# A decoder layer in float32: the first attention's work per tile re-ordered over two tiles, its layer norm moved to ScalarE

## The chip, the cores and the metric

The kernel is one program on one core of a Trainium2 chip. The metric is the device time of an execution in microseconds (us), from launch to end; the profiler takes one execution apart into the instructions of each engine. The engines are TensorE (PE, its weight loads PEld), VectorE (DVE), ScalarE (ACT), GpSimd (POOL) and SyncE (SP, which issues most DMAs). They run side by side and wait for each other on semaphores; each runs its own instructions in the order in which they are written.

## The reference, cut to what matters

The layer works on x of 16 x 64 tokens by 512. It is an attention with 32 heads of 16 and a layer norm, a cross-attention with 32 heads of 128 and a layer norm, and a gated dense layer with a layer norm. Only the first attention is touched by the change:

```python
xq = rotary((x @ Wq).reshape(b, s, 32, 16))
xk = rotary((x @ Wk).reshape(b, s, 8, 16));  xv = (x @ Wv).reshape(b, s, 8, 16)
xk, xv = repeat(xk, 4, axis=2), repeat(xv, 4, axis=2)
scores = einsum('bqhd,bkhd->bhqk', xq, xk) / sqrt(16)
probs = softmax(where(causal, scores, -inf), axis=-1)
x = layernorm(x + einsum('bhqk,bkhd->bqhd', probs, xv).reshape(b, s, 512) @ Wo)
```

Every product is computed to near float32 by splitting each operand into a rounded high part and the low rest and adding three products (high x high, high x low, low x high).

## The kernel before

**Tiles and steps.** The first attention runs over eight tiles of 128 tokens (two sequences of 64). Tile i's scores fall in four units of 512 columns (u = 0 to 3); two PSUM banks hold them, so units 0 and 1 are computed together, and then 2 and 3. The steps of one tile, with the names of the code:

- PE: `a_stage` turns the input tile over (four 128x128 transposes), `b_stage` multiplies by Wq (12 matmuls of 512 columns), `kv_stage` by Wk and Wv (12 of 256). `qk_stage` turns the rotated queries and keys over, six groups of four transposes (q, q, k, q, q, k) in three banks by turns. `s_stage` makes the scores of two units. `pt_stage` turns the probabilities of one unit over, `pv_stage` makes one half of the products with the values (24 matmuls of 256 for both halves), `wo_stage` multiplies by Wo (12 of 512), `x1_stage` turns the normed result over for the second attention.
- DVE: `rope_q` and `rope_k` (three instructions each) do the rotary products out of PSUM; `masked_max` is a COPY_PREDICATED that takes the masked scores out of PSUM and a TENSOR_REDUCE for the maxima; `total` is the sum of the exponentials and a RECIPROCAL; `add1` adds the residual from the bank of `wo_stage`; `stats1`, `moments1` and `norm1` are the layer norm; every `..._low` subtracts a high part from its source (L1379): `x_low`, `q_low` (1024 columns), `p_low` of one unit, `at_low` of the value products, `x1_low`.
- ACT: the high parts (all L885): `x_high`, the six copies of `qk_stage`'s banks, `p_high`, `at_high`, the 1024-column copy of the queries that feeds `q_low`, `x1_high`; and the exponentials (L923).
- POOL: `sub` (score minus maximum), `norm` (times the reciprocal), the two sums that end the rotary step (`t1q + t2q`, L1234, and the same for k), the low part of the keys (L1241) and of the values (L1252), and the inverse root of the norm (`root1`).
- SP: loads and the shuffling of the values.

**What sets the order.** No planner: each engine has a function `tile_steps(i)` written out by hand, with semaphore waits in front of each step. Work of three tiles stands in it: i (named `i`), v = i - 1 and w = i - 2. Tiles 0, 1 and 7 are unrolled and tiles 2 to 6 are a hardware loop. In PE's `tile_steps(i)` the steps stand as b(i), pt(v,0), pt(v,1), kv(i), pt(v,2), pt(v,3), a(i+1), qk(i), scores(i; 0,1), pv(v) in full, x1(w), scores(i; 2,3), wo(v). Behind tile 7 comes a hand-written passage into the second attention: pt(7,0), pt(7,1), four query products of the second attention (48 matmuls of 256 columns), pt(7,2), pt(7,3), pv(7), wo(7) and so on; the second attention's 32 units and the dense layer follow.

## Time and profile before

| | us |
|---|---|
| median of 3 runs (lowest to highest) | 824.31 (824.14 to 825.51) |
| the profiled execution, its own time | 824.27 |
| its span, first to last instruction | 822.5 |
| mean granted TensorE clock, share of full speed | 0.988 |
| busy over the span: PE / PEld | 765.3 (93%) / 691.1 (84%) |
| busy: DVE / POOL / ACT | 623.6 (76%) / 391.8 (48%) / 319.4 (39%) |

The busy shares are averages over stages that differ. The first attention takes the stretch from about 20 to 186 us; the rest belongs to the loads ahead of it and the two later stages. PE's busy time is modelled from pipelined matmuls, so a stretch can read as busy while its matmuls start later than they could; the start times of steps tell more than the busy column.

### The profile page before, as it was taken

To read this page: it belongs to the slowest core of one execution; us is meant where nothing else is said; L and a number is where in the kernel's file an instruction comes from. 1 tells how busy PE (TensorE), PEld (TensorE's weight loads), DVE (VectorE), ACT (ScalarE), POOL (GpSimd) and SP (SyncE) were. 2 spreads that over 40 slices of the span, in tenths; PEclk is the share of its full clock that TensorE was granted. 3 is DMA by queue.
4 is the path that set the end of the run, shared out by engine and by line. 5 is a ranking of instruction groups with operands and counts; after the bars stand their busy time and mean duration, and the time that the engine had idled before them with its cause. 6 is when DMAs were issued, how large, how long until landed. Compare 5 with 4: busy or idle time off the path is not lost.

```text
span 822.5 us, 15514 instructions
## 1 busy us (share of the span) xinstructions
PE 765.3 (93%) x5520; PEld 691.1 (84%) x5520; DVE 623.6 (76%) x1179; ACT 319.4 (39%) x669; POOL 391.8 (48%) x415
## 2 busy tenths in 40 slices
PE   3689999989899999999999999999999999998894
PEld 2677777779899998999999899999989999997773
DVE  4678888877887777678677767767776777788767
ACT  4455555562443323333332333333232333324313
POOL 7566666664544354444445444544444454443102
PEclk9899999999999999999999999999999999999998
DMA  9500004012333222123322212322221322131002
GB/s 256 124 18 17 16 16 118 3 55 52 85 104 96 52 78 78 27 58 84 87 51 77 77 26 66 84 79 51 77 77 26 75 82 73 45 84 27 1 1 103
DMA packets 104048, 53.50 MB, mean 65 GB/s; under 512 B 80208, under 2 KB 89552, under 8 KB 104016
## 3 DMA queue, kind: packets, MB, share of 16 engines
q1 hardware_dynamic: 103184, 51.51, 24.0%
q10 hardware_dynamic: 576, 1.05, 0.4%
q0 software_dynamic: 256, 0.52, 0.2%
q8 instruction: 19, 0.31, 0.2%
q14 instruction: 13, 0.11, 0.0%
HBM read 32.62 MB, written 2.10 MB: 42 GB/s over the span
## 4 chain that ended last, share of the span: by engine, by line
PE 70%; DVE 15%; issue 8%; POOL 3%; ACT 2%; DMA 1%; SPq 1%; DVEq 0%; ACTq 0%; POOLq 0%
PE bank L424 30%; PE bank L651 18%; PE s_bank L665 4%; DVE arena_r L1379 4%; PE bank L474 2%; PE s_bank L667 2%; PE bank L635 2%; PE bank L498 2%; DVE small L1467 2%; DVE arena_f L1461 1%; PE s_bank L635 1%; POOL arena_f L1295 1%; PE s_bank L498 1%; DMA arena_f<-in_L_attn_Wo 1%; PE bank L618 1%
## 5 line engine op out<-in xcount | busy, mean ns | idle before, releaser
L424 PE MATMUL bank<-arena_r 128*128 128x256 f32 (+1 forms) x2496 | 334.6, 290 | 2.8 <-DVE arena_r L1379 2.0
L424 PEld LDWEIGHTS bank<-arena_r 128*128 128x128 f32 x2496 | 313.3, 191 | 14.3 <-issue 2.4
L885 ACT ACTIVATE arena_r<-bank 128x256 fp32r<-128x256 f32 (+2 forms) x250 | 105.4, 459 | 227.7 <-PE bank L618 98.1
L651 PE MATMUL bank<-arena_r 128*128 128x512 f32 x768 | 191.5, 398 | 0.0
L651 PEld LDWEIGHTS bank<-arena_r 128*128 128x128 f32 x768 | 139.7, 189 | 27.3 <-DVE arena_r L1379 0.6
L1379 DVE TENSOR_TENSOR arena_r<-bank,arena_r 128x256 fp32r<-128x256 f32 (+2 forms) x218 | 100.3, 487 | 57.8 <-ACT arena_r L885 57.6
L885 ACT ACTIVATE arena_r<-arena_f 128x512 fp32r<-128x512 f32 (+2 forms) x178 | 103.8, 637 | 85.6 <-DMA arena_f<-arena_f 71.5
L1379 DVE TENSOR_TENSOR arena_r<-arena_f,arena_r 128x512 fp32r<-128x512 f32 (+1 forms) x114 | 115.9, 1030 | 19.1 <-ACT arena_r L885 19.0
L1262 POOL TENSOR_TENSOR arena_f<-arena_f 128x256 f32<-128x256 f32 x64 | 54.2, 846 | 91.6 <-DVE arena_f L1539 91.5
L1290 POOL TENSOR_TENSOR arena_f<-arena_f,small 128x512 f32<-128x512 f32 x32 | 33.4, 1044 | 109.9 <-DVE small L1602 109.9
L1295 POOL TENSOR_TENSOR arena_f<-arena_f,small 128x512 f32<-128x512 f32 x32 | 44.0, 1375 | 64.7 <-DVE small L1608 64.7
L1565 DVE TENSOR_TENSOR arena_f<-bank,arena_f 128x512 f32<-128x512 f32 x64 | 43.9, 686 | 24.2 <-PE bank L651 24.2
L885 ACT ACTIVATE arena_f<-s_bank 128x512 f32<-128x512 f32 (+1 forms) x35 | 20.5, 586 | 100.2 <-PE s_bank L667 92.6
L667 PE MATMUL s_bank<-arena_r 128*128 128x64 f32 x256 | 57.9, 244 | 0.0
L665 PE MATMUL s_bank<-arena_r 128*128 128x128 f32 x256 | 57.3, 295 | 0.0
L885 ACT ACTIVATE arena_r<-s_bank 128x512 fp32r<-128x512 f32 (+1 forms) x99 | 52.2, 528 | 1.1 <-PE s_bank L498 0.7
L1263 POOL TENSOR_TENSOR arena_f<-arena_f 128x256 f32<-128x256 f32 x64 | 50.1, 783 | 0.0
L667 PEld LDWEIGHTS s_bank<-arena_r 128*128 128x128 f32 x256 | 49.0, 191 | 1.2
L665 PEld LDWEIGHTS s_bank<-arena_r 128*128 128x128 f32 x256 | 49.0, 191 | 1.2
L1216 POOL TENSOR_TENSOR arena_f<-arena_f,small 128x512 f32<-128x512 f32 x32 | 34.3, 1072 | 32.8 <-DVE small L1463 32.8
L1596 DVE TENSOR_TENSOR arena_f<-s_bank,arena_f 128x512 f32<-128x512 f32 x32 | 22.1, 691 | 36.5 <-ACT arena_f L885 36.5
L1379 DVE TENSOR_TENSOR arena_r<-s_bank,arena_r 128x512 fp32r<-128x512 f32 (+1 forms) x83 | 47.8, 576 | 1.1 <-ACT arena_r L885 0.9
(147 smaller groups left out, 1065.2 us busy)
## 6 DMA issues: line engine op xcount, KB each, us to landing
arena_f<-arena_f SPq DMA_DIRECT2D x128, 128.0 KB, 2.5
arena_f<-in_L_xattn_Wq SPq DMA_DIRECT2D x8, 1024.0 KB, 5.5
arena_f<-in_L_xattn_Wo SPq DMA_DIRECT2D x8, 1024.0 KB, 5.5
arena_f<-in_x SPq DMA_DIRECT2D x8, 256.0 KB, 2.9
arena_f<-in_x SPq DMA_DIRECT2D x1, 2048.0 KB, 15.4
arena_f<-in_L_xattn_Wk SPq DMA_DIRECT2D x8, 256.0 KB, 3.0
arena_f<-in_L_xattn_Wv SPq DMA_DIRECT2D x8, 256.0 KB, 3.3
arena_f<-in_ctx SPq DMA_DIRECT2D x8, 256.0 KB, 3.1
```

Source lines behind the costliest of these rows:

```text
L424: mm = pe.matmul(bank, lhs(a, c), rhs(b, c), start=(c == 0 and n == 0), stop=(c == chunks - 1 and n == 2))
L651: mm = pe.matmul(BO2[i][:], at2[a][:, h, i * P:(i + 1) * P], w2o_s[b][:, h, :], start=(h == 0 and n == 0), stop=(h == HG - 1 and n == 2))
L665: pe.matmul(BS2[h][:, at:at + 2 * S], high, kT2[:, :, b * S:(b + 1) * S], start=True, stop=False, skip_group_check=True)
L667: mm = pe.matmul(BS2[h][:, at + S:at + 2 * S], low_, kT2[:, 0, b * S:(b + 1) * S], start=False, stop=True, skip_group_check=True)
L885: act.activation(dst, src, ACT.Copy).then_inc(done, 1)
L1216: pool.tensor_tensor(cut(p1[u], b=8, k=S), cut(sc1[u % 2], b=8, k=S), bcast(mx1[u], 2, S), ALU.subtract).then_inc(s_sub, 1)
L1262: pool.tensor_tensor(u1q[:, 0, j, :], u1q[:, 0, j, :], u2q[:, 1, j, :], ALU.subtract).then_inc(c_qs, 1)
L1263: pool.tensor_tensor(u1q[:, 1, j, :], u1q[:, 1, j, :], u2q[:, 0, j, :], ALU.add).then_inc(c_qs, 1)
L1290: pool.tensor_tensor(cut(p2, b=8, k=S), cut(sc2, b=8, k=S), bcast(mx2, 2, S), ALU.subtract).then_inc(c_sub, 1)
L1295: pool.tensor_tensor(cut(p2, b=8, k=S), cut(p2, b=8, k=S), bcast(sm2, 2, S), ALU.mult).then_inc(c_pn, 1)
L1379: dve.tensor_tensor(dst, src, f32(high), ALU.subtract).then_inc(done, 1)
L1565: dve.tensor_tensor(y, banks[6 + i][:], y, ALU.add).then_inc(c_acc, 1)
```

## The change

All four `tile_steps` are written in another order. On PE, tile i now runs qk(i), scores(i; 0,1), pt(v,2), pt(v,3), the first half of pv(v), scores(i; 2,3), the second half of pv(v), b(i+1), kv(i+1), x1(w), pt(i,0), pt(i,1), a(i+2), wo(v). So the projections of a tile stand at the end of the tile before it, and the last two probability units and the value products of v stand among the scores of i. `x1_stage` gets bank 7 (the bank of the value products) in place of bank 2, and waits for `at_low(v)`. `qk_stage` uses its three banks in another turn, so that the bank that `add1` reads is its third; its wait for `add1(i-2)` moves to the third group. The norm's scaling moves from DVE to ACT for tiles 0 to 5 (a new POOL instruction makes -mean x rstd); tiles 6 and 7, in the passage behind, keep it on DVE. Tile 2 and tile 6 are unrolled too; the loop is tiles 3 to 5. Ahead of tile 0 stand b(0), kv(0), a(1) and tile 0's rotary steps. The passage behind tile 7 is as before.

```diff
             def kv_stage(t, first):
                 if first:
                     pe.wait_ge(s_w1l, EC + 1)
+                else:
+                    pe.wait_ge(s_rk, t)
...
-            QK = (TX, TR[0], TR[1])
+            QK = (TR[0], TR[1], TX)
 
             def qk_stage(t, first):
                 pe.wait_ge(s_ql, t + 1)
-                if tile_stages(t)[2]:
-                    pe.wait_ge(s_res, t - 1)
                 for j, (kind, n) in enumerate((("q", 0), ("q", 1), ("k", 0), ("q", 2), ("q", 3), ("k", 1))):
                     if j == 2:
                         pe.wait_ge(s_kl, t + 1)
+                        if tile_stages(t)[2]:
+                            pe.wait_ge(s_res, t - 1)
                     if j >= 3:
                         pe.wait_ge(s_qke, 6 * t + j - 2)
-                    elif j > 0 and not first:
-                        pe.wait_ge(s_pl, 4 * t - 2 + j)
+                    elif j < 2 and not first:
+                        pe.wait_ge(s_pl, 4 * t - 3 + j)
...
-            def x1_stage(w, i, bank=BKV):
+            def x1_stage(w, bank):
                 pe.wait_ge(s_x1n, w + 1)
-                if i is not None:
-                    pe.wait_ge(s_rk, i + 1)
-                    pe.wait_ge(s_vr, i + 1)
...
                 start = not old
-                b_stage(i, start)
-                if old:
-                    pt_stage(v, 0)
-                    pt_stage(v, 1)
-                if old:
-                    pe.wait_ge(s_cp, 4 * i)
-                kv_stage(i, start)
+                qk_stage(i, start)
+                s_stage(i, (0, 1), start)
                 if old:
                     pt_stage(v, 2)
                     pt_stage(v, 3)
-                if following:
-                    pe.wait_ge(s_rq, i + 1)
-                    a_stage(i + 1)
-                qk_stage(i, start)
-                s_stage(i, (0, 1), start)
-                if old:
+                    if oldest and not starts_with(w):
+                        pe.wait_ge(s_x1l, w)
                     pv_stage(v, 0, not oldest)
-                    pv_stage(v, 1, not oldest)
-                if oldest:
-                    x1_stage(w, i)
-                if start:
+                else:
                     table_turn()
                 s_stage(i, (2, 3), start)
+                if old:
+                    pv_stage(v, 1, not oldest)
+                if following:
+                    b_stage(i + 1, False)
+                    kv_stage(i + 1, False)
+                if oldest:
+                    pe.wait_ge(s_al, v + 1)
+                    x1_stage(w, BO)
+                if following:
+                    pt_stage(i, 0)
+                    pt_stage(i, 1)
+                if has_tile(i + 2):
+                    pe.wait_ge(s_rq, i + 2)
+                    a_stage(i + 2)
                 if old:
                     wo_stage(v, i, not oldest)
...
+            def norm1(w):
+                act.wait_ge(s_lp, 2 * w + 2)
+                if not starts_with(w):
+                    act.wait_ge(s_x1T, w)
+                act.activation(x1n, res[:, bass.ds(w, 1), :].rearrange("p t n -> p (t n)"), ACT.Identity,
+                               bias=nmean1, scale=rstd).then_inc(s_x1n, 1)
...
+                if old:
+                    p_high(v, 2, not oldest)
+                    p_high(v, 3, not oldest)
                 if not following:
-                    wq_high(0, 2)
-                    wq_high(0, 3)
-                if old:
-                    at_high(v, not oldest)
+                    wq_high(0, 0)
+                    wq_high(0, 1)
                 expo(i, 0)
                 if not old:
                     table_copy(0)
                     table_copy(1)
                 expo(i, 1)
+                if oldest:
+                    norm1(w)
+                if old:
+                    at_high(v, not oldest)
                 act.wait_ge(d_v, 64 * (i + 1))
                 if old:
                     act.wait_ge(s_pv, i)
                 copy(v_blocks(vpad[0]), v_st, s_vh)
-                if oldest:
-                    act.wait_ge(s_x1n, w + 1)
-                    copy(res[:, bass.ds(w, 1), :].rearrange("p t n -> p (t n)"), x1n, s_x1c)
-                    x1_high(w)
                 if not following:
+                    wq_high(0, 2)
+                    wq_high(0, 3)
                     wkv_high(0, 0)
                     wkv_high(0, 1)
                 expo(i, 2)
                 expo(i, 3)
+                if following:
+                    p_high(i, 0, not old)
+                    stack_q_high(i + 1)
+                    p_high(i, 1, not old)
+                    v_out(i + 1)
+                    stack_k_high(i + 1)
+                if has_tile(i + 2):
+                    x_high(i + 2)
+                if oldest:
+                    copy(res[:, bass.ds(w, 1), :].rearrange("p t n -> p (t n)"), x1n, s_x1c)
+                    x1_high(w, banks[7])
...
+                pool.wait_ge(s_lp, 2 * w + 1)
+                pool.sem_inc(s_hold, 1)
+                pool.tensor_scalar(nmean1, mv[:, 0:1], rstd, -1.0, ALU.mult, ALU.mult).then_inc(s_lp, 1)
...
                 if oldest:
                     root1(w)
                 sub(i, 0, not old)
                 sub(i, 1, not old)
                 norm(i, 0)
+                if not following:
+                    wq_low(0, 0)
+                    wq_low(0, 1)
+                sub(i, 2, not old)
                 pool.wait_ge(s_vh, i + 1)
                 pool.tensor_tensor(v_blocks(vpad[1]), v_st, f32(v_blocks(vpad[0])),
                                    ALU.subtract).then_inc(s_vl, 1)
-                sub(i, 2, not old)
                 norm(i, 1)
                 sub(i, 3, not old)
+                if following:
+                    sum_q1(i + 1)
+                    norm(i, 2)
+                    sum_k1(i + 1)
+                    norm(i, 3)
...
-                dve.copy_predicated(sc, bcast(causal[:], 1, 8), cut(banks[5 + u % 2][:], b=8, k=S)).then_inc(s_cp, 1)
+                dve.copy_predicated(cut(sc1[u % 2], b=8, k=S), bcast(causal[:], 1, 8),
+                                    cut(banks[5 + u % 2][:], b=8, k=S)).then_inc(s_cp, 1)
+
+            def maximum(v, u):
                 dve.wait_ge(s_cp, 4 * v + u + 1)
-                dve.tensor_reduce(mx1[u], sc, AX.X, ALU.max).then_inc(s_mx, 1)
+                dve.tensor_reduce(mx1[u], cut(sc1[u % 2], b=8, k=S), AX.X, ALU.max).then_inc(s_mx, 1)
...
-                if old:
-                    total(v, 2)
-                rope_q(i, not old)
-                if old:
-                    total(v, 3)
-                    p_low(v, 0)
-                    p_low(v, 1)
-                rope_k(i, not old)
-                if not old:
-                    for h in range(HG):
-                        dve.wait_ge(s_w1oh, h + 1)
-                        low(w1out[1][:, h, :], w1out_raw[:, h, :], w1out[0][:, h, :], s_w1ol)
                 if oldest:
                     add1(w)
-                q_low(i)
+                if following:
+                    x_low(i + 1)
+                if oldest:
+                    stats1(w)
+                    moments1(w)
+                masked(i, 0, not old)
+                masked(i, 1, not old)
+                maximum(i, 0)
                 if old:
                     p_low(v, 2)
                     p_low(v, 3)
-                if oldest:
-                    stats1(w)
-                if following:
-                    x_low(i + 1)
-                if oldest:
-                    moments1(w)
-                masked_max(i, 0, not old)
-                if oldest:
-                    norm1(w)
-                masked_max(i, 1, not old)
+                maximum(i, 1)
+                masked(i, 2, not old)
+                maximum(i, 2)
+                total(i, 0)
                 if not following:
                     wq_low(0, 2)
+                masked(i, 3, not old)
+                maximum(i, 3)
+                total(i, 1)
+                if following:
+                    rope_q(i + 1, False)
                 if old:
                     at_low(v)
-                total(i, 0)
-                masked_max(i, 2, not old)
-                total(i, 1)
+                if following:
+                    total(i, 2)
+                    rope_k(i + 1, False)
+                    p_low(i, 0)
+                    p_low(i, 1)
+                    q_low(i + 1)
+                    total(i, 3)
+                else:
+                    wq_low(0, 3)
                 if oldest:
-                    x1_low(w)
+                    x1_low(w, banks[7])
                 if not following:
-                    wq_low(0, 3)
                     add1(v)
-                masked_max(i, 3, not old)
```

How this stands in the programs. First PE between one tile's output projection and the next scores, before the change (bank1 takes b and a, bank2 kv, bank3 and s_bank the probabilities' and keys' transposes, bank0 the first group of qk and wo):

```order
L443 MATMUL bank1<-arena_r 128x512 x12
L462 MATMUL bank3<-ident,arena_f 128x128 x4
L462 MATMUL s_bank<-ident,arena_f 128x128 x4
L424 MATMUL bank2<-arena_r 128x256 x12
L462 MATMUL bank3<-ident,arena_f 128x128 x4
L462 MATMUL s_bank<-ident,arena_f 128x128 x4
L434 MATMUL bank1<-ident,arena_f 128x128 x4
L498 MATMUL bank0<-ident,arena_r 128x128 x4
```

and after it, from the second half of the value products on (L541 is `x1_stage`, L472 `pt_stage`, L508 `qk_stage`):

```order
L484 MATMUL bank7<-arena_r 128x256 x12
L448 MATMUL bank1<-arena_r 128x512 x12
L429 MATMUL bank2<-arena_r 128x256 x12
L541 MATMUL bank7<-ident,arena_f 128x128 x4
L472 MATMUL bank3<-ident,arena_f 128x128 x4
L472 MATMUL s_bank<-ident,arena_f 128x128 x4
L439 MATMUL bank1<-ident,arena_f 128x128 x4
L429 MATMUL bank0<-arena_r 128x512 x12
L508 MATMUL bank3<-ident,arena_r 128x128 x4
```

`x1_stage` now stands between the projections and the probabilities' transposes, and bank 0 is written by the output projection immediately ahead of the next tile's qk.

DVE up to a tile's first masked scores, before the change (tile 7; L1432 is `add1`, 128x32x32 is `q_low`, then `p_low` of units 2 and 3 and the norm's statistics):

```order
L1407 TENSOR_TENSOR arena_f<-bank2,rope1 128x128
L1409 SCALAR_TENSOR_TENSOR arena_f<-bank2,rope1 128x64
L1410 TENSOR_TENSOR arena_f<-bank2,rope1 128x64
L1432 TENSOR_TENSOR arena_f<-bank0,arena_f 128x512
L1379 TENSOR_TENSOR arena_r<-arena_f,arena_r 128x32x32
L1379 TENSOR_TENSOR arena_r<-bank3,arena_r 128x2x2x128
L1379 TENSOR_TENSOR arena_r<-s_bank,arena_r 128x2x2x128
L1437 BN_STATS small<-arena_f 128x6
L1442 BN_AGGR small<-small 128x2
L1444 TENSOR_SCALAR small<-small 128x1
L1461 COPY_PREDICATED arena_f<-causal,s_bank 128x512
```

and after it, for the same tile (L1517 and L1519 are `total`, 128x4x128 out of bank7 is `x1_low`, L1480 is `add1`):

```order
L1427 TENSOR_TENSOR arena_r<-arena_f,arena_r 128x32x32
L1517 TENSOR_REDUCE small<-arena_f 128x8
L1519 RECIPROCAL small<-small 128x8
L1427 TENSOR_TENSOR arena_r<-bank7,arena_r 128x4x128
L1480 TENSOR_TENSOR arena_f<-bank0,arena_f 128x512
L1485 BN_STATS small<-arena_f 128x6
L1490 BN_AGGR small<-small 128x2
L1492 TENSOR_SCALAR small<-small 128x1
L1508 COPY_PREDICATED arena_f<-causal,s_bank 128x512
```

`add1` stood ahead of the query's low part; now it stands behind it, with a `total` and `x1_low` between.

The low part of the value products (128x512 out of bank7) on DVE, before, in tile 7 (L1448 is `norm1`, 128x4x2x64 a low part of Wq for the second attention):

```order
L1461 COPY_PREDICATED arena_f<-causal,s_bank 128x512
L1463 TENSOR_REDUCE small<-arena_f 128x8
L1448 TENSOR_SCALAR arena_f<-arena_f,small 128x512
L1461 COPY_PREDICATED arena_f<-causal,bank6 128x512
L1463 TENSOR_REDUCE small<-arena_f 128x8
L1379 TENSOR_TENSOR arena_r<-arena_f,arena_r 128x4x2x64
L1379 TENSOR_TENSOR arena_r<-bank7,arena_r 128x512
```

and after, in the same tile, from the third mask on:

```order
L1508 COPY_PREDICATED arena_f<-causal,s_bank 128x512
L1513 TENSOR_REDUCE small<-arena_f 128x8
L1517 TENSOR_REDUCE small<-arena_f 128x8
L1519 RECIPROCAL small<-small 128x8
L1427 TENSOR_TENSOR arena_r<-arena_f,arena_r 128x4x2x64
L1508 COPY_PREDICATED arena_f<-causal,bank6 128x512
L1513 TENSOR_REDUCE small<-arena_f 128x8
L1517 TENSOR_REDUCE small<-arena_f 128x8
L1519 RECIPROCAL small<-small 128x8
L1427 TENSOR_TENSOR arena_r<-bank7,arena_r 128x512
```

It stood behind two masks and two maxima; now all four masks and maxima, two totals and a low part of Wq are ahead of it. In the other tiles `rope_q` of the next tile is ahead of it in place of Wq's.

## Rows read from the trace of the kernel before

**Rows 1.** Stretches: us, busy of PE, PEld, DVE, ACT, POOL; PEclk, DMA, GB/s.
```profile
67.71:169.25 101.54, 92.22 (x697) 79.14 (x696) 90.18 (x177) 60.19 (x113) 66.22 (x67) 1.00 0.14 34
88.06:108.39 20.33, 18.53 (x142) 15.93 (x142) 18.00 (x36) 11.90 (x23) 12.83 (x13) 1.00 0.08 16
```

**Rows 2.** Timeline, PE, one tile: start, us, engine, line, operation [idle before].
```profile
93.70 3.00 PE L424 MATMUL bank<-arena_r 128*128 128x512 f32 x12
96.53 2.89 PE L443 MATMUL bank<-arena_r 128*128 128x512 f32 x12
99.26 0.60 PE L462 MATMUL bank<-ident,arena_f 128*128 128x128 f32 x4
100.05 1.68 PE L424 MATMUL bank<-arena_r 128*128 128x256 f32 x12
102.49 0.65 PE L462 MATMUL bank<-ident,arena_f 128*128 128x128 f32 x4 [0.76 <-DVE arena_r L1379]
105.20 1.26 PE L498 MATMUL bank<-ident,arena_r 128*128 128x128 f32 x8 [0.75 <-DVE arena_r L1379]
108.39 0.29 PE L522 MATMUL s_bank<-arena_r 64*128 64x64 f32 x1
109.40 3.12 PE L474 MATMUL bank<-arena_r 128*128 128x256 f32 x24
```

**Rows 3.** Timeline, DVE, the same tile.
```profile
92.88 0.69 DVE L1379 TENSOR_TENSOR arena_r<-bank,arena_r 128x512 fp32r<-128x512 f32 x1 [0.18 <-ACT arena_r L885]
98.10 0.69 DVE L1463 TENSOR_REDUCE small<-arena_f 128x8 f32<-128x512 f32 x1
98.70 0.68 DVE L1467 TENSOR_REDUCE small<-arena_f 128x8 f32<-128x512 f32 x1
99.58 0.69 DVE L1396 TENSOR_TENSOR arena_f<-bank,rope 128x512 f32<-128x512 f32 x1
100.85 0.68 DVE L1467 TENSOR_REDUCE small<-arena_f 128x8 f32<-128x512 f32 x1
103.93 1.22 DVE L1379 TENSOR_TENSOR arena_r<-arena_f,arena_r 128x1024 fp32r<-128x1024 f32 x1
109.71 0.75 DVE L1461 COPY_PREDICATED arena_f<-causal,s_bank 128x512 f32<-128x512 int32 x1 [0.44 <-PE bank L522]
110.49 0.69 DVE L1463 TENSOR_REDUCE small<-arena_f 128x8 f32<-128x512 f32 x1
```

**Rows 4.** Timeline, POOL, the same tile.
```profile
94.48 1.04 POOL L1221 TENSOR_TENSOR arena_f<-arena_f,small 128x512 f32<-128x512 f32 x1 [0.58 <-DVE small L1469]
95.48 0.74 POOL L1252 TENSOR_TENSOR arena_r<-arena_f,arena_r 128x256 fp32r<-128x256 f32 x1
96.17 1.05 POOL L1216 TENSOR_TENSOR arena_f<-arena_f,small 128x512 f32<-128x512 f32 x1
101.02 1.29 POOL L1234 TENSOR_TENSOR arena_f<-arena_f 128x512 f32<-128x512 f32 x1
```

**Rows 5.** Timeline, ACT, the same tile.
```profile
92.25 0.60 ACT L885 ACTIVATE arena_r<-bank 128x512 fp32r<-128x512 f32 x1 [2.85 <-PE bank L474]
102.42 1.06 ACT L885 ACTIVATE arena_r<-arena_f 128x1024 fp32r<-128x1024 f32 x1 [0.87 <-POOL arena_f L1234]
103.38 0.58 ACT L885 ACTIVATE arena_r<-bank 128x512 fp32r<-128x512 f32 x1
```

**Rows 6.** Timeline, PE: tile 1's first scores; then the passage behind tile 7.
```profile
47.58 0.29 PE L522 MATMUL s_bank<-arena_r 64*128 64x64 f32 x1
...
180.70 5.99 PE L424 MATMUL bank<-arena_r 128*128 128x256 f32 x48
186.53 0.60 PE L462 MATMUL bank<-ident,arena_f 128*128 128x128 f32 x4
```

**Rows 7.** Stretches, PE alone: us, busy (instructions), PEclk, DMA, GB/s.
```profile
18.00:19.00 1.00, 0.00 (x0) 0.50 1.05 350
23.37:28.39 5.02, 5.02 (x24) 0.54 0.71 123
```

121 lines of the change are left out of this document (68 added, 53 removed).

## Prediction

> **What bounds the kernel now.** I read the page's shares first, then the stretches by tile, then the timeline of one tile engine by engine, then the passage behind tile 7. The reader should see that in the first attention two engines are nearly full, and that neither is full: from the first scores of tile 2 to those of tile 7, 101.54 us for five tiles, 20.31 each, PE is busy 92.22 and DVE 90.18; in one tile of 20.33 PE has 18.53 and DVE 18.00 [rows 1]. So a tile is a ring of waits through both, not one engine's queue. In the timeline PE stands 0.76 ahead of a probability transpose and 0.75 ahead of qk, each time for DVE [rows 2]. The ring closes on DVE: from the first masked scores to q_low some 14.5 us of nearly unbroken work, and from q_low's start (103.93) to the next masked scores (109.71) 5.78: q_low to qk 1.27 (103.93 to 105.20), qk 3.19 (to 108.39), scores to mask 1.32 [rows 2, 3]. 14.55 + 5.78 is the period. The change can win only what it takes out of this ring, not what it hides elsewhere.
>
> **Unit prices**, start to start, for a queue that doesn't wait. DVE: mask 0.78 (109.71 to 110.49), a 512-column reduction, low part or add 0.60 (98.10 to 98.70), a total with its reciprocal 0.88 (to 99.58), rope_q 1.27 (to 100.85), q_low 1.13, rope_k 0.46 [rows 3]; the last two are busy times less the overlap of about 0.09 that the others show. PE: b 2.73 (96.53 to 99.26), wo 2.83 (93.70 to 96.53), four transposes 0.43, kv 1.35 (its 1.68 less the modelled tail), half of pv 1.49, a pair of scores 1.0 (108.39 to 109.40) [rows 2]. POOL: sub or norm 1.00, values' low part 0.69, sum of q 1.23 [rows 4]. Hand-overs: ACT copy to DVE low part 0.63 (92.25 to 92.88), at_low to PE 0.82 (92.88 to 93.70), transposes to ACT copy 0.89 (102.49 to 103.38), POOL's sum to ACT's 1024-column copy 1.40 (101.02 to 102.42), that copy to the next ACT instruction 0.96 [rows 2 to 5].
>
> **The steady tile after the change.** Zero is the first mask; the first scores then start at -1.32 and PE is free at -0.31. DVE runs four masks (3.12), four maxima (2.40), p_low of units 2 and 3 (1.20) and two totals (1.76) without a wait that I can find, so rope_q starts at 8.48 and at_low at 9.75. PE runs two transposes, half of pv, scores, waits 0.5 for p_low 3, second half, b and kv and is through at 9.1. There x1 waits for at_low: 9.75 + 0.82 = 10.57. That is 1.5 us of new PE idle, and queued behind it are the transposes of units 0 and 1 (11.1, 11.5), a(i+2) and wo (12.4 to 15.2). On ACT the copy of unit 0 starts at 12.0, the 1024-column copy at 12.53, the copy of unit 1 at 13.5; on DVE p_low 1 at 14.13, q_low at 14.73. The 1024-column copy has a second reason to be there: POOL's norm 0 starts at 6.35 (total 0 with its reciprocal), then sub 2, values, norm 1 and sub 3 stand ahead of the sum of q: 6.35 + 1.00 + 1.00 + 0.69 + 1.00 + 1.00 = 11.04, and + 1.40 = 12.44. So the ring to q_low is 14.7, about what it was (14.55): DVE has less work ahead of q_low, and gets waits of 0.9 twice in its place. wo hides the hand-over only in part: qk can start at 14.73 + 1.27 = 16.0, where PE is free at 15.2.
>
> Then the moved wait. The third group of qk needs add1 of the tile two back, and on DVE that add stands behind q_low, a total and x1_low: 14.73 + 1.13 + 0.88 + 0.60 = 17.34; + 0.8 hand-over is 18.15, where the group could have started at 16.86. Fourth and fifth group follow at 0.43 each; the sixth needs the third one's copy out of bank 0 (0.69 + 0.60 + 0.1 behind 18.15, so 19.5); its four transposes and the switch to the scores take 0.57, so first scores at 20.1, next mask at 21.4. Without the add the scores would start 3.05 behind qk, and the tile would be 16.0 + 3.05 + 1.32 = 20.4. The period is 21.4 against 20.31: +1.1 a tile. What the norm's move to ACT takes off DVE (0.54 busy) lies in idle time of DVE ahead of the mask (19.5 to 21.4), so it counts nothing; the same holds for the new POOL instruction (its cost isn't in the trace; between 0.1 and 1.4, and POOL is idle there), and ACT has room (11.90 of 20.33).
>
> **First tiles.** Until the first scores of tile 0 (28.39, the end of the stretch in [rows 7]) nothing on the path moves. Tile 0 has no at_low and x1, but POOL's order holds: sum of q at about 40.2, ACT's copy 41.6, unit 1's copy 42.55, p_low 43.2, q_low 43.8, qk 45.05, scores of tile 1 at 48.1 against 47.58 [rows 6]: +0.5. Tile 1 to tile 2 has the add but no x1_low: 20.75 against 20.13, +0.6. Tiles 2 to 7, five periods: 5 x 21.42 = 107.1 against 101.54, +5.6. Tile 7's first scores are then 6.7 us late.
>
> **The passage.** Time again from tile 7's first mask. PE has no b and kv there: it is through with pv at 5.05 and stands at x1 until at_low. On DVE total 0 ends at 6.2; wq_low waits for ACT's third copy of Wq (two copies moved ahead of the exponentials, then at_high and values; ready 8.05), then mask, maximum and total: at_low at 10.9, x1 at 11.7. PE idle 6.7. Then wo (12.25 to 15.1), two transposes, the 48 query matmuls at 15.95 for 5.83 (180.70 to 186.53 in [rows 6]), pt(7,2) at 21.8, that is 23.1 behind the first scores. Before it was 186.53 - 169.25 = 17.28 [rows 1, 6]. So +5.8. Units 2 and 3 are ready by 18.1 and 19.5 even with both wq_low on POOL ahead of sub 2, under the query matmuls. Behind pt(7,2) both kernels are the same, and PE, being late, finds nothing to give back.
>
> **The clock.** While PE stood empty between 18 and 19 us the granted clock was 0.50, the lower level (1.2 GHz of 2.4), and tile 0's qk behind it, which takes 3.19 in a later tile, took 5.02 at 0.54: 1.8 more [rows 2, 7]. An idle of 6.7 us in the passage can do the same: 0 if the clock holds, 1.8 to 2.4 if not. I take 2.0. Of this the Trainium skill ("TensorE: Matmul & The Clock Gate", Part 1, on the clock gate) says that an idle TensorE is dropped to 1.2 GHz and regains 2.4 only by sustained work; the trace agrees with its 0.50. By that rule the 2.0 is due, without it the sum is 2 less.
>
> **Sum.** 0.5 + 0.6 + 5.6 + 5.8 + 2.0 = 14.5, on the profiled execution's 824.27 (the median of the runs, 824.31, is the same): 838.8. Its own range: the period +-0.5 over six tiles (+-3), passage +-1.5, clock -2: 833 to 843.
>
> **Rivals.**
> - The add isn't the last wait (it comes when I say, but total and x1_low find a gap, or the ring to q_low is 0.9 shorter). Then a tile is 20.4, +0.1, and 0.5 + 0.6 + 5.8 + 2 stay: 833. For it: add1 misses by only 1.3. Against: DVE's order is fixed.
> - Faster: the waits that I find between ACT, POOL and DVE overlap, and the tile falls to what PE is busy, 18.53 of 20.33 [rows 1]: six times -1.8, +0.5, half of the passage's 5.8: 817. It decides if at_low starts before kv is through, at 8.3 or earlier. For it: by the unit prices PE's work is only 2.73 + 2.83 + 1.35 + 11 x 0.43 + 2.98 + 2.0 + 0.5 = 17.1 a tile. Against: rope_q and two totals stand ahead of at_low.
> - Faster by the instruction alone: DVE is the bound and only norm1 counts, six times -0.46, 821.5. For it: DVE's 18.00 of 20.33. The Trainium skill ("VectorE: DVE Perf Modes", Rules for kernel authors) speaks for it: what counts on VectorE is the number of instructions, and one goes. Against: DVE has 2.3 idle in each tile, and gets more.
> - No change: new waits and saved ones cancel, 823 to 826.
> - Slower still: POOL's instructions stretch while DVE works beside them and the Wq parts delay the softmax past the query matmuls, 845.
>
> **Chances.** Forecast 0.60, add not last 0.16, faster by overlap 0.08, by the instruction 0.05, no change 0.05, still slower 0.06. A difference below 0.2% (1.6 us) can't be told from none here. So slower 0.82, same 0.05, faster 0.13. The range for 8 in 10 runs from 828 (leaving out the faster cases and no change) to 844.
>
> **What would show it.** Right: tiles 3 to 7 with a period near 21.4; on PE idle of about 1.5 ahead of x1 (L541) put down to at_low, of 0.8 ahead of qk and about 1.3 ahead of its third group, put down to add1 (L1480); in tile 7 some 6.7 idle ahead of L541 and a granted clock at half behind it. Wrong: a period under 20.3, or x1 without a wait.

## The result: 839.3 us, slower by 1.9%, and the profile after

| | before | after |
|---|---|---|
| median of the runs (lowest to highest), us | 824.5 (824.1 to 825.5), 4 runs | 839.3 (838.8 to 841.7), 4 runs |
| ratio, 95% interval | | 1.0186 (1.0168 to 1.0204) |
| span of the profiled execution | 822.5 | 837.3 |
| mean granted clock | 0.988 | 0.979 |

The prediction said 838.8 (828 to 844). The total is right to 0.5 us, and that closeness is luck: several parts are off and cancel, and in the profiled execution 1.7 of the 14.8 us lie in stretches that the forecast put at nothing. The stretches first, as in [rows 1]: five tiles from the scores of tile 2 to those of tile 7, one of them, and the passage from the middle of TensorE's idle time into what follows (us, busy of PE, PEld, DVE, ACT, POOL, clock, DMA, GB/s):

```profile
68.45:174.24 105.79, 91.62 (x697) 80.45 (x697) 85.61 (x169) 62.19 (x115) 68.01 (x71) 0.98 0.12 31
89.11:110.03 20.92, 18.12 (x142) 15.88 (x142) 17.30 (x34) 12.48 (x24) 13.54 (x15) 1.00 0.07 16
184.00:190.00 6.00, 2.85 (x9) 2.47 (x10) 3.63 (x7) 1.58 (x4) 5.60 (x5) 0.50 0.13 23
```

A tile takes 20.9 where it took 20.33 (the five periods are 20.66, 20.92, 22.45, 21.02 and 20.74), and DVE is less busy in it (17.30 against 18.00). PE's timeline of that tile (start, us, line, operation, idle before it and its releaser) shows three idle times, where [rows 2] has two:

```profile
97.91 1.59 PE L429 MATMUL bank<-arena_r 128*128 128x256 f32 x12
100.60 0.66 PE L541 MATMUL bank<-ident,arena_f 128*128 128x128 f32 x4 [1.11 <-DVE arena_r L1427]
102.33 2.99 PE L429 MATMUL bank<-arena_r 128*128 128x512 f32 x12
106.08 0.65 PE L508 MATMUL bank<-ident,arena_r 128*128 128x128 f32 x4 [0.76 <-DVE arena_r L1427]
108.10 1.09 PE L508 MATMUL bank<-ident,arena_r 128*128 128x128 f32 x8 [0.93 <-DVE arena_f L1480]
110.03 0.29 PE L532 MATMUL s_bank<-arena_r 64*128 64x64 f32 x1
```

The third is the moved wait: qk's third group behind `add1`. DVE's timeline beside it shows why the add is late: the queries' low part, the last total, x1's low part, then L1480.

```profile
104.73 1.22 DVE L1427 TENSOR_TENSOR arena_r<-arena_f,arena_r 128x1024 fp32r<-128x1024 f32 x1
105.86 0.68 DVE L1517 TENSOR_REDUCE small<-arena_f 128x8 f32<-128x512 f32 x1
106.75 0.69 DVE L1427 TENSOR_TENSOR arena_r<-bank,arena_r 128x512 f32 x1
107.36 0.68 DVE L1480 TENSOR_TENSOR arena_f<-bank,arena_f 128x512 f32 x1
```

PE's waits from 40 to 200 us (total, times, longest):

```profile
PE bank L541 <- DVE arena_r L1427: 12.0, 6, 6.7
PE bank L508 <- DVE arena_r L1427: 10.4, 7, 4.5
PE bank L508 <- DVE arena_f L1480: 5.1, 6, 1.1
```

Where the time went, from the starts of tiles' first scores in both traces ([rows 1, 6, 7] for before):

| stretch | before | after | difference | predicted |
|---|---|---|---|---|
| up to tile 0's scores | 28.39 | 27.71 | -0.7 | 0 |
| tile 0 to 1 | 19.19 | 20.60 | +1.4 | +0.5 |
| tile 1 to 2 | 20.13 | 20.14 | 0.0 | +0.6 |
| tiles 2 to 7 | 101.54 | 105.79 | +4.2 | +5.6 |
| tile 7's scores to pt(7,2) | 17.28 | 24.71 | +7.4 | +7.8 |
| behind pt(7,2) | 636.0 | 638.4 | +2.4 | 0 |
| span | 822.5 | 837.3 | +14.8 | +14.5 |

The start of tile 0 lay between 25.3 and 29.0 us in the fourteen profiles of this study, for reasons that no edit here explains, and the time behind pt(7,2), where all have the same code, between 636.0 and 639.2. So a single trace tells a difference of the whole span to no better than a few microseconds; the periods of tiles that keep their clock agree to 0.1 between traces of the same order.

In the passage, PE, then the two ACT and two POOL instructions that matter (on POOL subtraction 2, the values' low part and norm 1 run between the two), then DVE's low part of x1 and the add:

```profile
187.15 1.12 PE L541 MATMUL bank<-ident,arena_f 128*128 128x128 f32 x4 [6.73 <-DVE arena_r L1427]
187.91 4.27 PE L429 MATMUL bank<-arena_r 128*128 128x512 f32 x12
193.12 5.99 PE L429 MATMUL bank<-arena_r 128*128 128x256 f32 x48
```
```profile
189.63 0.63 ACT L938 ACTIVATE arena_f<-arena_f 128x512 f32<-128x512 f32 x1 [2.51 <-POOL arena_f L1252]
190.69 0.58 ACT L900 ACTIVATE arena_r<-bank 128x512 fp32r<-128x512 f32 x1
```
```profile
182.52 2.95 POOL L1315 TENSOR_TENSOR arena_r<-arena_f,arena_r 128x512 fp32r<-128x512 f32 x2
188.56 1.04 POOL L1252 TENSOR_TENSOR arena_f<-arena_f,small 128x512 f32<-128x512 f32 x1
```
```profile
191.30 0.69 DVE L1427 TENSOR_TENSOR arena_r<-bank,arena_r 128x512 fp32r<-128x512 f32 x1 [3.60 <-ACT arena_r L900]
192.22 0.69 DVE L1480 TENSOR_TENSOR arena_f<-bank,arena_f 128x512 f32<-128x512 f32 x1 [0.23 <-PE bank L429]
```

x1 is turned at 187.15, but its copy on ACT runs at 190.69, behind exponential 3, which waits for POOL's subtraction 3, late because two parts of Wq stand ahead of it. The add of tile 6 stands behind x1's low part on DVE, and here it also waits 0.23 for the slowed wo.

### The profile page after: what moved, and what is told of

It is laid out like the page before. It is cut to its first block, busy times and chain, and to the rows that moved or that the text cites. A ratio compares the mean times of both kernels' runs of the same rounds, so it can differ in the third digit from the quotient of the medians.

```text
span 837.3 us, 15423 instructions
## 1 busy us (share of the span) xinstructions
PE 769.2 (92%) x5520; PEld 697.3 (83%) x5520; DVE 618.4 (74%) x1173; ACT 323.8 (39%) x675; POOL 395.9 (47%) x423
## 4 chain that ended last, share of the span: by engine, by line
PE 65%; DVE 13%; issue 10%; POOL 8%; ACT 2%; DMA 1%; SPq 1%; DVEq 0%; ACTq 0%; POOLq 0%
PE bank L429 29%; PE bank L660 18%; DVE arena_r L1427 4%; PE s_bank L674 4%; POOL arena_f L1252 3%; PE s_bank L676 2%; PE bank L644 2%; PE bank L508 2%; POOL arena_f L1257 1%; PE s_bank L644 1%; POOL arena_f L1339 1%; DVE small L1513 1%; POOL arena_f L1269 1%; DMA arena_f<-in_L_attn_Wo 1%; PE bank L627 1%
## 5 line engine op out<-in xcount | busy, mean ns | idle before, releaser
L900 ACT ACTIVATE arena_r<-bank 128x256 fp32r<-128x256 f32 (+1 forms) x250 | 106.9, 460 | 227.6 <-PE bank L627 96.0
L900 ACT ACTIVATE arena_r<-arena_f 128x512 fp32r<-128x512 f32 (+1 forms) x178 | 103.7, 637 | 82.6 <-DMA arena_f<-arena_f 75.1
L1427 DVE TENSOR_TENSOR arena_r<-arena_f,arena_r 128x512 fp32r<-128x512 f32 (+1 forms) x114 | 115.2, 1024 | 22.9 <-ACT arena_r L900 22.8
L900 ACT ACTIVATE arena_f<-s_bank 128x512 f32<-128x512 f32 (+1 forms) x35 | 20.5, 586 | 100.4 <-PE s_bank L676 92.5
L1644 DVE TENSOR_TENSOR arena_f<-s_bank,arena_f 128x512 f32<-128x512 f32 x32 | 22.1, 691 | 36.5 <-ACT arena_f L900 36.5
```

Source lines behind the costliest of these rows:

```text
L900: act.activation(dst, src, ACT.Copy).then_inc(done, 1)
L1427: dve.tensor_tensor(dst, src, f32(high), ALU.subtract).then_inc(done, 1)
```

## The experiments

Ratios are against the kernel before, run beside each; each kernel has 4 to 12 executions. The ratios and the medians of two variants run at different times can differ by 1 to 2 us in what they say of the step between them; where they do, both are given.

### Is the add the last wait? (e1)

```diff
-                if oldest:
-                    add1(w)
                 if following:
                     x_low(i + 1)
...
                     q_low(i + 1)
+                    if old:
+                        add1(v)
                     total(i, 3)
```
Expected: 

> The changed kernel with one edit: on VectorE add1 of the tile before stands right behind q_low, ahead of the last total and x1_low. In the changed kernel the third group of qk waits 0.92 us for that add in a steady tile, 5.1 us in six waits. Theory (the add is the last wait, and what it costs goes on to the next scores): the six waits of 5.1 us go and nothing takes their place, so 5 to 6 us faster than the changed kernel, about 833.5 to 834.5 (ratio to the kernel before 1.011 to 1.012), with periods near 20.0 in place of 20.7. Rival (the scores are held by the copies between qk's groups, or the last total becomes late for ScalarE): the wait goes and the period stays, 838.5 to 840.

Measured: 831.9, ratio 1.0097 (1.0083 to 1.0110), 7 us less than the changed kernel and 1.6 below the range that was expected. The wait for L1480 is gone and no other wait for DVE has grown; PE's waits from 40 to 200 us and the five tiles:

```profile
PE bank L541 <- DVE arena_r L1427: 12.0, 6, 6.7
PE bank L508 <- DVE arena_r L1427: 10.3, 7, 4.5
```
```profile
66.80:166.54 99.74, 90.12 (x697) 78.96 (x697) 85.51 (x169) 61.74 (x115) 67.95 (x70) 1.00 0.13 34
```

The period is 19.95, below the 20.31 of before. So the new order of the tile is in itself a small gain, and this one wait turned it into a loss. It gave 6.05 in five tiles, more than its five waits of 0.9: in the changed kernel one of the five periods was 22.45, with a granted clock of 0.62 behind the broken idle time ahead of the third group; in e1 no tile had that. That stretch of the changed kernel:

```profile
128.50:133.00 4.50, 3.99 (x26) 3.66 (x26) 1.99 (x5) 2.57 (x5) 1.31 (x3) 0.62 0.90 272
```

### Does x1's wait carry the tile? (e8)

```diff
-                if following:
-                    rope_q(i + 1, False)
                 if old:
                     at_low(v)
                 if following:
+                    rope_q(i + 1, False)
                     total(i, 2)
```
Expected: 

> The changed kernel with one edit: on VectorE at_low stands ahead of the three instructions of rope_q (1.25 us). In the changed kernel TensorE waits 12.0 us in six waits for at_low ahead of x1, 6.7 of them in tile 7, where there is no rope_q. The other five (1.1 each) go. Theory of the prediction (the ring to q_low has a second support, GpSimd's sum of q, which starts at the same time in both, and the add still stands behind q_low): the wait at x1 goes and TensorE waits as much longer ahead of qk; the period stays within 0.2 and the kernel at 838 to 840. Rival (x1 carries the units' transposes and so the ring): -1.1 in each of six tiles, 832.5 to 834.

Measured: 840.5, ratio 1.0196 (1.0180 to 1.0213): no gain. The profiled execution was the longest of the six, 846.6, with a fallen clock in four of its five periods (22.1 to 22.8); the fifth, at full clock, took 20.72 against 20.66 in the changed kernel. PE's waits from 40 to 200 us:

```profile
PE bank L508 <- DVE arena_r L1427: 16.0, 7, 4.5
PE bank L541 <- DVE arena_r L1427: 5.3, 1, 5.3
PE bank L508 <- DVE arena_f L1480: 4.4, 6, 1.1
```

The five waits at x1 are gone and the wait ahead of qk grew by what they held. In the tile at full clock DVE's rope_q ends before POOL's sum of q (L1269) starts:

```profile
79.51 0.41 DVE L1447 TENSOR_TENSOR arena_f<-bank,rope 128x256 f32<-128x256 f32 x1
79.63 1.05 POOL L1252 TENSOR_TENSOR arena_f<-arena_f,small 128x512 f32<-128x512 f32 x1
80.63 1.30 POOL L1269 TENSOR_TENSOR arena_f<-arena_f 128x512 f32<-128x512 f32 x1
```

The sum waits for nothing but POOL's own queue. So the prediction's claim of a second support for the ring (POOL's sum of q) holds: the first of the three idle times costs nothing by itself.

### The norm, in either order (e3, b1)

e3 takes the norm back to VectorE in the changed kernel, b1 moves it to ScalarE in the kernel before:

```diff
# e3, ScalarE and then VectorE
-                if oldest:
-                    norm1(w)
...
                 maximum(i, 0)
+                if oldest:
+                    norm1(w)
```
Expected of e3: 

> The changed kernel with the norm of the second sublayer's input back on VectorE, behind the first maximum (0.54 us busy there). The prediction counted its move to ScalarE at nothing, since VectorE has idle time ahead of the mask. Here it comes back behind the mask, ahead of at_low, where no wait lies: by the prediction's own ring this costs 0.46 x 6 = 2.8 us if at_low and then ScalarE's copy and q_low pass it on (842), and nothing if the ring to q_low is set by GpSimd's sum of q, as the prediction's second support had it (839.3). Rival (ScalarE is what binds, and the norm burdens it more): 1 to 3 us faster than the changed kernel.

Expected of b1: 

> The kernel before with one part of the change: the norm of the second sublayer's input on ScalarE in place of VectorE, with GpSimd's short instruction for its bias; nothing is moved otherwise (ScalarE's loop over the middle tiles of the first attention is written out). Theory (in the kernel before the ring from mask to q_low is nearly unbroken VectorE work, so an instruction less counts in full): six times -0.46, 821.5 or so, ratio 0.996 to 0.998. Rival (a hand-over closes the gap, as the wait of 0.75 ahead of qk only moves): 824, ratio 0.999 to 1.001. It tells what of the change's +15 belongs to the norm.

Measured: e3 843.0, ratio 1.0225 (1.0212 to 1.0239), 3 to 4 us more than the changed kernel; its five tiles took 108.70 against 105.79, one of them 23.42 with a fallen clock, the others 21.1 to 21.5. b1 824.0, ratio 0.9997 (0.9986 to 1.0008), period 20.33 as before. So the same instruction is worth nothing in the old order and 0.5 to 0.6 a tile in the new one. b1's theory fell: although DVE is busy 18.00 of 20.33, one instruction less on it moved nothing. Its trace shows why, in the high part of the value products on ACT and the low part on DVE:

```profile
90.56 0.60 ACT L886 ACTIVATE arena_r<-bank 128x512 fp32r<-128x512 f32 x1 [1.21 <-PE bank L475]
91.19 0.69 DVE L1392 TENSOR_TENSOR arena_r<-bank,arena_r 128x512 fp32r<-128x512 f32 x1 [0.65 <-ACT arena_r L886]
```

at_low starts 3.50 behind the tile's first mask in both kernels (b1's first mask is at 87.69, the one of before in that tile at 89.38); before it waited 0.18 for the high part ([rows 3]), in b1 0.65. The high part waits for TensorE's value products in both. So the stretch of the old ring from the mask to at_low ran through TensorE and ScalarE, and not through VectorE's queue alone as the prediction had it.

### The passage (e2)

```diff
                 total(i, 0)
                 if not following:
-                    wq_low(0, 2)
+                    at_low(v)
...
+                if not following:
+                    wq_low(0, 2)
```
Expected: 

> The changed kernel with one edit, in tile 7 alone: on VectorE at_low stands right behind the first total, and Wq's third low part, which waits 1.62 us for ScalarE's copy, stands behind it. In the changed kernel TensorE is idle for 6.73 us ahead of x1 there, and wo behind it takes 4.27 us at half clock. Theory (the passage is held by the order on VectorE): at_low starts some 4 us earlier, x1's wait falls to about 3, the pt of tile 7 comes 3 to 4 us earlier and, if the clock also holds, 2 more: 833.5 to 836. Rival (Wq's parts, the norms on GpSimd or the units' sums bind behind x1): the wait at x1 falls, but the idle comes back ahead of the query matmuls or of pt: 838.5 to 840.

Measured: 841.5, ratio 1.0219 (1.0196 to 1.0243): the rival, 1.5 above its range. PE in the passage:

```profile
183.53 0.66 PE L541 MATMUL bank<-ident,arena_f 128*128 128x128 f32 x4 [2.55 <-DVE arena_r L1427]
183.94 4.58 PE L429 MATMUL bank<-arena_r 128*128 128x512 f32 x12
193.40 8.27 PE L429 MATMUL bank<-arena_r 128*128 128x256 f32 x48 [3.43 <-issue]
```

Counted from the tile's first scores (174.81 here), x1 came 4.2 us earlier, at 8.7 in place of 12.9, and the query matmuls only 0.3 earlier, at 18.6. The idle time was only moved behind wo, and there it cost the clock under the 48 query matmuls: 0.50 granted from 193.4 to 197, 8.27 us for 5.99.

### Does the passage's idle time cost by the clock? (e4)

```diff
+                if not following:
+                    for _ in range(12):
+                        for c in range(4):
+                            pe.transpose(TX[:, c * P:(c + 1) * P], ident[:], ident[:])
                 if oldest:
                     pe.wait_ge(s_al, v + 1)
```
Expected: 

> The changed kernel with one addition: 48 transposes of the identity into bank 0, whose contents aren't used, on TensorE in tile 7 ahead of the wait for at_low; TensorE isn't idle for 6.73 us there but for some 1.5. Nothing else is changed. In the changed kernel the granted clock was 0.50 from 184 to 190 us and wo took 4.27 us where it takes 2.83 at full clock. Theory (the idle time costs the clock, as the prediction's 2.0 us had it): x1 starts when it did, 187.2, wo takes about 2.9 and the query matmuls start 0.7 to 1.5 us earlier unless ScalarE's and VectorE's copies for them come last: 1 to 2 us faster than the changed kernel, 837.3 to 838.3. Rival (what holds the query matmuls is not TensorE: the copies of x1 stand on ScalarE behind exponential 3): 0, about 839.3.

Measured: 837.8, ratio 1.0176 (1.0150 to 1.0202). The median lies in the theory's range, but the five executions spread from 835.3 to 841.9 and aren't told apart from the changed kernel; what decides is the trace. PE, then DVE:

```profile
181.17 5.40 PE L577 MATMUL bank<-ident 128*128 128x128 f32 x48
188.08 0.66 PE L541 MATMUL bank<-ident,arena_f 128*128 128x128 f32 x4 [1.51 <-DVE arena_r L1431]
188.49 3.00 PE L429 MATMUL bank<-arena_r 128*128 128x512 f32 x12
193.89 5.98 PE L429 MATMUL bank<-arena_r 128*128 128x256 f32 x48 [1.53 <-issue]
```
```profile
192.24 0.69 DVE L1431 TENSOR_TENSOR arena_r<-bank,arena_r 128x512 fp32r<-128x512 f32 x1 [3.61 <-ACT arena_r L904]
192.84 0.68 DVE L1484 TENSOR_TENSOR arena_f<-bank,arena_f 128x512 f32<-128x512 f32 x1
```

The clock stayed up and wo took 3.00 in place of 4.27. The query matmuls still start 18.74 behind the tile's first scores (18.88 in the changed kernel). They wait for tile 6's add (the second DVE row), which stands behind x1's low part, that behind x1's copy on ACT, and that behind exponential 3. What the clock lost there had been hidden, all but 0.14 of it: from tile 0's scores to pt(7,2) e4 takes 171.5 and the changed kernel 171.2.

### The passage in full, and the tile in full (f1, f2, g1)

f1 is e1 with tile 7 reordered on three engines: at_low behind the first total; Wq's first copies and low parts at the tile's start; x1's copies ahead of exponential 3. f2 then reorders the steady tile (`k_low1` is the last instruction of `sum_k1`, made a step of its own):

```diff
# f2: GpSimd
                 norm(i, 1)
-                sub(i, 3, not old)
                 if following:
                     sum_q1(i + 1)
-                    norm(i, 2)
                     sum_k1(i + 1)
-                    norm(i, 3)
+                sub(i, 3, not old)
+                if following:
+                    k_low1(i + 1)
+                    norm(i, 2)
+                    norm(i, 3)
# f2: ScalarE
-                expo(i, 3)
                 if following:
                     p_high(i, 0, not old)
-                    stack_q_high(i + 1)
                     p_high(i, 1, not old)
-                    v_out(i + 1)
+                    stack_q_high(i + 1)
                     stack_k_high(i + 1)
+                expo(i, 3)
+                if following:
+                    v_out(i + 1)
# f2: VectorE: at_low, rope_q, rope_k, total(i, 2), p_low 0 and 1, q_low
```
Expected of f1: 

> e1_add_early (add1 behind q_low, 831.9) with the passage behind tile 7 reordered, after what e2_at7 showed (x1 came 3.6 us earlier, and its copies then stood on ScalarE behind exponential 3, that behind GpSimd's subtraction 3, and that behind the two Wq parts): in tile 7 alone at_low stands behind the first total on VectorE, Wq's first two copies on ScalarE ahead of the copies of qk, their low parts on GpSimd at the start of the tile, where it is idle, and the copies of x1 ahead of exponential 3. Theory (the passage is held by the order on these three engines): x1 at 9 behind the tile's first scores in place of 12.9, the query matmuls at 14 to 15 in place of 18.7, so 4 to 5 us faster than e1: 827 to 828. Rival (the Wq parts or TensorE's clock bind): the query matmuls move less than 1.5, 830.5 to 832.

Expected of f2: 

> f1_passage with the steady tile reordered too: on VectorE at_low, rope_q, rope_k, then the third total; on GpSimd the sums of q and k ahead of subtraction 3, k's low part ahead of norms 2 and 3; on ScalarE the copies of units 0 and 1 and then q's and k's ahead of exponential 3. From e1's tile (period 20.0; at_low 117.48, last copy's low part 121.73, q_low 122.34, qk 123.69, k's low part to 124.70, third group 124.83): at_low 1.25 earlier, x1 without a wait, q_low at 120.6 to 121, qk at 122, k's low part to 123.2, third group 123.5. Theory (the three chains that meet in qk move together): period 18.7 to 19, where TensorE is full, tile 0 some 2 shorter, so 8 to 10 us faster than f1: 818 to 820, faster than the kernel before. Rival (a chain that I don't see closes the gap, such as exponential 3 and the norms): period 19.7 to 20, 825 to 828.

Expected of g1, which is f2 with the add late again: 

> f2_full (819.7 us) with add1 put back where the changed kernel has it, behind q_low, the last total and x1_low on VectorE. It asks whether the prediction's step on the add holds where the rest of the tile is shorter. In f2 qk starts at 119.69, its third group at 120.84 without a wait, and q_low ends at 119.5; the add would then start at 119.5 + 0.9 + 0.6 = 121.0, the third group at 121.8 in place of 120.84. Theory (the add is the last wait): +1.0 in six tiles, and the clock may fall in some of them: 825.5 to 828, period 19.7. Rival (at this period TensorE's own work takes it up): 819 to 821.

Measured: f1 829.7, ratio 1.0076 (1.0062 to 1.0089). In its trace the query matmuls start 14.7 behind tile 7's scores (18.7 in e1), 4.0 earlier as expected, but the medians differ by 2.1 only. It lies between the theory's range and the rival's. Tile 0's start and the time behind pt(7,2) were 1.6 and 0.9 longer in that trace; where the rest of the 4.0 goes in the other executions is open. f2 819.7, ratio 0.9957 (0.9940 to 0.9974), faster than before. Its five tiles:

```profile
67.04:160.84 93.80, 91.07 (x698) 78.66 (x697) 85.54 (x169) 62.14 (x117) 67.23 (x72) 1.00 0.15 38
```

18.76 a tile, with PE busy 18.2 of them: this is the tile of the rival of 817, to which the prediction gave 0.08 for the change itself. g1 827.6, ratio 1.0032 (1.0021 to 1.0044): the late add alone costs 7.9 in the shorter tile by the medians, 6.2 by the ratios. The period was 20.1 in most tiles and the six waits sum to 8.1:

```profile
PE bank L508 <- DVE arena_f L1492: 8.1, 6, 1.8
```

### Idle time that does cost the clock (f3, f4, f5)

f3 is f2 with a fill (transposes of the identity whose result nobody reads) in tile 0. f4 is f3 with the passage tightened further: in tile 7 the high part of the value products ahead of the norm on ScalarE, all four Wq copies early, and the add ahead of x1's low part on VectorE. f5 is f4 with a fill of 16 in the passage. The edit of f3:

```diff
+            def fill(n):
+                for m in range(n):
+                    pe.transpose(TX[:, (m % 4) * P:(m % 4 + 1) * P], ident[:], ident[:])
...
                     pt_stage(i, 0)
+                    if isinstance(i, int) and i == 0:
+                        fill(16)
                     pt_stage(i, 1)
                 if has_tile(i + 2):
                     pe.wait_ge(s_rq, i + 2)
                     a_stage(i + 2)
+                if isinstance(i, int) and i == 0:
+                    fill(20)
```
Expected of f3: 

> f2_full with 36 transposes of the identity into bank 0, contents unused, in the two idle times of TensorE in tile 0 (2.0 us ahead of the second unit's transposes, 2.6 us ahead of the next tile's qk); nothing else is changed. In f2 the granted clock was 0.55 to 0.50 from 42 to 48 us, and qk to the first scores took 5.31 us where a later tile takes 4.0. Theory (the idle time costs the clock and the work behind it is on the path, unlike in the passage of e4): the clock stays at 1.00, qk to scores 4.0 to 4.3, 1.0 to 1.4 us faster than f2, 818.4 to 818.7. Rival (GpSimd's low part of k binds qk's third group anyway): qk to scores stays over 5 us, 819.7.

Expected of f4: 

> f3_warm0 with the passage tightened: in tile 7 ScalarE makes at_high ahead of the norm and all four Wq copies early, and on VectorE the add of tile 6 stands ahead of x1_low. In f2 the query matmuls start 14.3 us behind tile 7's first scores and wait 1.19 for that add; before it was 11.4. Theory: at_low 0.7 earlier, wo with it, the add at once behind wo: query matmuls at 13 to 13.3, so 1.0 to 1.4 faster than f3: 817.0 to 817.7. Rival (the Wq low parts on VectorE or GpSimd's norm 1 come last): within 0.4 of f3.

Expected of f5: 

> f4_best with 16 more transposes of the identity into bank 0, contents unused, on TensorE in tile 7 ahead of the wait for at_low. In f4 TensorE is idle for 1.93 us there, the granted clock falls to half, and wo behind it takes 4.58 us where it takes 3.0 at full clock; the query matmuls start at 168.81, 0.67 behind the last unit's transposes. In e4 the same fill kept the clock, and nothing came of it, since the add of tile 6 stood behind the copies of x1. In f4 the add stands ahead of them. Theory (wo and the add now carry the passage): wo in 3.0, query matmuls 1.2 to 1.6 earlier, 813.7 to 814.1 against f4's 815.3. Rival (Wq's low parts on VectorE or norm 1 on GpSimd come last): an idle time of 1 or more ahead of the query matmuls, 815.

Measured: f3 814.5, ratio 0.9871 (0.9855 to 0.9887), less than f2 by 5 us (medians) or 7 (ratios), where 1.0 to 1.4 was expected. PE ahead of tile 1's qk in f2:

```profile
43.28 1.12 PE L508 MATMUL bank<-ident,arena_r 128*128 128x128 f32 x4 [2.58 <-DVE arena_r L1439]
```
and in f3:
```profile
38.71 2.35 PE L546 MATMUL bank<-ident 128*128 128x128 f32 x20
41.45 0.66 PE L508 MATMUL bank<-ident,arena_r 128*128 128x128 f32 x4 [0.40 <-DVE arena_r L1447]
```

From qk's start to the scores f2 takes 5.31, f3 3.07; I had put the latter at 4.0. That is 2.2 of the gain. The spans of the two traces differ by 4.7, but 1.8 of that lies ahead of tile 0's scores, where the code is the same; tiles 2 to 7 take 93.8 in both. The other 3 or more are therefore open: f2's twelve executions had mean clocks from 0.978 to 0.987 and times from 817.2 to 823.9, f3's four all 0.988 and 813.4 to 815.3, and only one execution of each was profiled. That the fill in tile 0 keeps later tiles from losing their clock is a guess.

f4 815.3, ratio 0.9886 (0.9871 to 0.9902), and f5 816.0, ratio 0.9884 (0.9864 to 0.9904): no better than f3, and nearer the rival in both. In the traces pt(7,2) comes 149.9 behind tile 0's scores in f3, 149.3 in f4, 148.3 in f5, so each did a part of what was meant. In f5 wo takes 3.01 again and 0.59 of idle time is left ahead of the query matmuls, whose add now follows two low parts of Wq. The executions do not tell a microsecond apart.

## Why the prediction was right, and where it was not

- **The ring of the new order and its price: right, 0.5 too long.** Of the steps of a tile, counted from its first mask (90.43 in the tile shown), x1 came at 10.17 (10.57 predicted), q_low at 14.30 (14.73), qk at 15.65 (16.0), its third group at 17.67 (18.15), the next mask at 20.91 (21.4). Nearly the whole error is in the first step, DVE's four masks, maxima and totals up to at_low. What the prediction had wrong is the ring of before: it closed it on DVE alone, and b1 showed that at_low waited there for TensorE's value products. The sum didn't use that.
- **The add as the last wait: right, and shown twice.** Rival "the add isn't the last wait" is out: e1 took 7 us off, g1 put 6 to 8 on. Its twin, 20.4 a tile without the add, was close too (19.95).
- **The second support by POOL: right** (e8).
- **"What the norm's move takes off DVE counts nothing": wrong as it stood.** The step weighed it against idle time ahead of the mask. But the norm stood behind the first maximum, ahead of at_low, and there its absence is worth 3 to 4 us in all in the new order (e3). The sum was not hurt, since the ring had been added up without the norm. The rival "by the instruction alone" is out too: in the order of before an instruction less on VectorE told nothing (b1, 0.9997). The Trainium skill ("VectorE: DVE Perf Modes", Rules for kernel authors) advises to minimize the number of operations; it doesn't say that each one less shortens a kernel, and here it did so only in the new order.
- **First tiles: the sum right (1.1 predicted, 1.4 measured), the parts not.** All of it fell between tiles 0 and 1, where the granted clock was 0.50 from 41 to 47 us, in and behind 4.5 us of idle time. The 0.6 forecast for tiles 1 to 2 did not come. The prediction had a clock term for the passage alone.
- **The passage, 5.8, and its clock, 2.0: right sum, wrong parts.** x1's idle time is 6.73 for 6.7. But the query matmuls started 1.6 later than forecast (18.88 behind the scores, 17.27 by the prediction: its 15.95 and 1.32). The step that failed is the one that took them as free once wo was through: their add stands behind x1's low part, and x1's copy behind exponential 3. And the clock term, 2.0, was worth 0.14 (e4, in the trace): the clock did fall to half as forecast and wo took 4.27, but its loss fell into that same wait. Measured, the two terms came to 7.4 in place of 7.8. Of the 7.4 the reordered passage of f1 took 4.2 back and that of f5 5.9 (pt(7,2) 20.5 and 18.8 behind the scores, in place of 24.7); the last 1.6 against the kernel before is open.
- **Not forecast: 2.4 behind pt(7,2).** 1.7 of it lies in the dense stage, where both kernels have the same code: the difference grew from 13.9 (784.80 against 770.94, the end of its first group of matmuls) to 15.5 at the last matmul (827.13 against 811.60). Behind an idle time of 2.6 in both, the clock was at half from 788 to 794.6 after, and from 775.8 to 779 before. After, and then before:

```profile
788.00:794.60 6.60, 6.60 (x34) 5.57 (x33) 3.99 (x11) 3.75 (x15) 0.00 (x0) 0.50 0.00 0
```
```profile
775.80:779.00 3.20, 3.20 (x19) 2.44 (x18) 2.27 (x6) 2.59 (x10) 0.00 (x0) 0.51 0.00 0
```

It is not a cost of the change that any run here pins down: e4, the changed kernel with the fill alone, took 636.0 behind pt(7,2), as the kernel before did. So the five periods were forecast 1.4 and the passage 0.4 too long, the first tiles 0.3 and the end 2.4 too short, and tile 0 started 0.7 early. From tile 0's scores to pt(7,2), where all the terms of the forecast lie, the change cost 13.1 where 14.5 was forecast; the rest of the agreement is luck.

## What to carry to other kernels

When a wait is moved, look at what stands ahead of the instruction that ends it, in that instruction's own queue: here one residual add behind a total and a low part cost 7 us, and the same reordering without it was a gain. Removing one idle time of a ring moves it to the next one as long as a second chain ends there at the same time; only when all chains that meet (queries, keys, the add) were moved together did the tile fall from 20.0 to 18.8. And a stretch that drains the pipeline, such as the last tile, wants its own order: an order that is right while the next tile's projections fill TensorE leaves it empty without them.

## What the runs showed of the hardware

- Short idle times broken by a little work can cost the clock as one long one can: 0.76 and 0.92 us idle with 1.1 us of transposes between were followed by a granted clock of 0.62 in one tile of five (the changed kernel), and 0.76 and 0.93 in another tile by none. In e8, with 1.9 to 2.2 and 0.4 to 1.1 idle, four of the five periods were 22.1 to 22.8 in the profiled execution, and the fifth, with 1.86 and 0.81, was 20.7.
- The same idle time need not have the same effect: 2.57 us in tile 7 was followed by a wo of 4.54 in f1 and of 3.01 in f2, and 1.93 us by a wo of 4.58 in f4.
- Transposes of a constant into a bank that nobody reads at the time kept the granted clock at 1.00 each time (e4, f3, f5). They gained time only where the work behind was on the path: 2.2 us in tile 0 by the trace, 0.14 in the passage of e4.
- Two low parts of 128x512 on GpSimd took 2.95 in one piece where VectorE ran a like part of Wq beside them, and that part took 1.28 in place of 0.69. At the same place without it they took 2.53 (e2), and at the tile's start 2.52 (f1).
